# State-space recurrence: rows spread eight at a time from blocks laid out by GpSimd, squares and end scaling on ScalarE, inputs over three segments

## The reference, cut to what matters

```python
def step(h, inp):
    dA_t, dB_t, x_t, C_t, t = inp
    h = h * dA_t + dB_t * x_t[:, :, None]
    nrm = jnp.sqrt(jnp.sum(h * h, axis=(1, 2), keepdims=True))
    fac = jnp.minimum(20.0 / (nrm + 1e-08), 1.0)
    h = jnp.where(t % 10 == 0, h * fac, h)
    y = jnp.einsum('bdn,bn->bd', h, C_t) + D_param * x_t
    return (h, y)
```

## Time and profile before

| | |
|---|---|
| device time, 3 runs | 6174.59, 6184.56 (median), 6189.38 us |
| the profiled execution | 6185.92 us, of which the core's span is 6184.0 us |
| granted TensorE clock over the span | 0.867 of 2.4 GHz |
| PE, PEld, DVE, ACT, POOL busy in the span | 81%, 52%, 52%, 48%, 31% |
| the recurrence | 4094.8 to 4634.6 us after the span's start, about 540 us |
| first scan, last scan (53 in all) start | 4112.03, 4599.13 us |

### The profile page before, as it was taken

One profiled execution on the slowest core, in us unless ns is written; L12 is line 12 of the kernel. 1 busy time (PEld: TensorE's weight loads), 2 busy tenths in 40 slices (PEclk: granted clock), 3 DMA queues, 4 the chain that ended last, 5 costly groups with the idle time before them and its releaser, 6 DMA issues. The chain is left out here.

```text
span 6184.0 us, 108311 instructions
## 1 busy us (share of the span) xinstructions
PE 5032.6 (81%) x39346; PEld 3240.5 (52%) x39346; DVE 3189.3 (52%) x6332; ACT 2957.8 (48%) x8829; POOL 1901.8 (31%) x2082
## 2 busy tenths in 40 slices
PE   3998598978878878878788788778989944787888
PEld 2664255756636546546456456458886632223433
DVE  5551354556546446455356366358875544562433
ACT  2442244547647657556467477355534412352421
POOL 0230000347637457367277187001112300000000
PEclk6999799999989989899899799776669966895888
DMA  1000000001101111111111011000000000000000
GB/s 48 2 1 4 19 10 16 1 14 39 47 19 41 40 29 36 35 34 35 31 39 41 25 40 41 32 1 1 1 1 5 1 3 4 10 4 29 4 0 7
DMA packets 34520, 122.70 MB, mean 20 GB/s; under 512 B 8484, under 2 KB 9512, under 8 KB 32424
## 3 DMA queue, kind: packets, MB, share of 16 engines
q1 hardware_dynamic: 33960, 115.42, 6.9%
HBM read 36.43 MB, written 1.05 MB: 6 GB/s over the span
## 5 line engine op out<-in xcount | busy, mean ns | idle before, releaser
L640 POOL MEMSET norm_eps<- 128x1 f32 x16 | 1.6, 99 | 1905.7 <-POOLq L116 1847.2
L2087 POOL TENSOR_TENSOR local_rot<-local_raw,local_cos 128x512 f32<-128x512 f32 x384 | 488.1, 1271 | 303.5 <-DVE local_raw L2131 303.5
L2090 POOL TENSOR_TENSOR local_other<-local_raw,local_sin 128x256 f32<-128x256 f32 x768 | 557.6, 726 | 60.2
L2029 ACT ACTIVATE ps<-ps,local_negmax 128x96 f32<-128x96 f32 x1536 | 489.2, 322 | 37.2 <-DVE local_negmax L2110 36.9
L1952 PE MATMUL ps<-arena,local_xs 128*128 128x512 f32 x768 | 447.4, 667 | 71.8 <-ACT local_xs L2009 52.0
L2093 POOL TENSOR_TENSOR local_rot<-local_rot,local_other 128x512 f32<-128x512 f32 x384 | 487.4, 1269 | 30.1
L2024 ACT ACTIVATE local_squares<-ps 128x512 f32<-128x512 f32 x384 | 230.8, 601 | 508.2 <-PE ps L1952 507.8
L2117 DVE TENSOR_REDUCE local_norm<-local_squares 128x8 f32<-128x512 f32 x384 | 263.2, 685 | 282.4 <-ACT local_squares L2024 282.4
L1940 PE MATMUL ps<-local_K,local_Q 64*64 64x96 f32 x6144 | 337.0, 249 | 0.0
L2029 ACT ACTIVATION_READ_ACCUMULATOR ps<-ps,local_negmax 128x1 f32 x1536 | 331.0, 215 | 0.0
L2519 PE MATMUL ps<-ssm_BC,const 32*128 32x40 f32 (+1 forms) x3584 | 297.8, 373 | 26.4 <-PEq L116 22.0
(11 more groups left out here) (499 smaller groups left out, 11465.9 us busy)
## 6 DMA issues: line engine op xcount, KB each, us to landing
local_V_span<-local_V SPq DMA_DIRECT2D x96, 384.0 KB, 4.0
local_V_span<-local_V SPq DMA_DIRECT2D x96, 256.0 KB, 3.5
arena<-in_L1f_a SPq DMA_DIRECT2D x7, 2176.0 KB, 8.2
local_V_span<-local_V SPq DMA_DIRECT2D x72, 128.0 KB, 2.3
arena<-in_L3f SPq DMA_DIRECT2D x1, 3460.0 KB, 11.6
arena<-in_L1f_f SPq DMA_DIRECT2D x6, 537.5 KB, 4.0
arena<-in_L0f SPq DMA_DIRECT2D x1, 2824.5 KB, 9.8
arena<-in_L0x SPq DMA_DIRECT2D x1, 2049.5 KB, 9.0
```

The lines of the kernel that those rows point to most:

```text
L2029: nc.scalar.activation(scores, scores, ACT.Exp, bias=m.negmax[:, s % 2, u:u + 1], accum_out=m.total[:, s % 2, u:u + 1])\
L2087: link(nc.gpsimd.tensor_tensor(rot, raw, m.cos[:, t, a * DH:(a + 1) * DH].unsqueeze(1) .broadcast_to([P, 8, DH]), ALU.mult))
L2090: link(nc.gpsimd.tensor_tensor(other[:, :, lo:lo + HALF], raw[:, :, HALF - lo:DH - lo], m.sin[:, t, a * DH + lo:a * DH + lo + HALF].unsque ...
```

## The change

1. Spreading. GpSimd lays out, per chunk, four blocks of 8 rows x 40 tokens (`own`): block (kind, h) holds row n of `BC` in partition n of each sequence's 32 and zeros elsewhere (a product of `BC` with `own_row`, a tiled identity of 32; both operands broadcast). A use is then 2 matmuls of 32 x 128 by 320 columns, with ones as weights, in place of 16 of 40 columns.
2. The squares go from VectorE to ScalarE (L2588 after), and so does the scaling of the ends by `fac` (L2602 after: 4 instructions of 32 elements, one for each sequence). VectorE computes the product of ends and first decay before the factor is known (`pre`, L2699 after) and multiplies it with `fac` afterwards (L2720 after).
3. The B uses are spread in steps 0, 0, 1, 2 and their 16 takes stand in steps 1, 2, 3 as 4, 6, 6 (before: 8 in step 2, 8 in step 3). The C uses are spread in steps 2 and 3, three in 3; ScalarE copies one in step 3 and three in step 0 of the next chunk (before: all four in step 3).
4. The decays of a chunk are made in quarters (8 Tanh, Exp of 1280, two small ones), one in each step, the first of chunk k+2 in step 3 of chunk k. Before they stood in one piece at the start of a chunk.
5. In step 0 the second weighing product stands behind the reduction, and y of half 0 waits for it as before. In the other steps both stand ahead of it, as before. The second y input reads, and the `y_ready` waits of takes, follow half by half.

The diff, cut to its core:

```diff
+    sq, scratch, pre = buf("sq", [P, B, DN]), buf("scratch", [P, B, DN]), buf("pre", [P, B, DN])
...
-        return {1: [("B", k + 1, 0, 0), ("B", k + 1, 0, 1)], 2: [("B", k + 1, 1, 0), ("B", k + 1, 1, 1)],
-                3: [("C", k + 1, h, p) for h in range(2) for p in range(2)]}.get(i, [])
+        return [(kind, k + 1, h, p) for kind, h, p in
+                {0: [("B", 0, 0), ("B", 0, 1)], 1: [("B", 1, 0)], 2: [("B", 1, 1), ("C", 0, 0)],
+                 3: [("C", 0, 1), ("C", 1, 0), ("C", 1, 1)]}[i]]
...
+    TAKES = 0, 4, 6, 6
...
         def _(pe):
...
-                        for n in range(HALF):
-                            for b in range(2):
-                                part = slice(32 * (2 * p + b), 32 * (2 * p + b) + 32)
-                                row = 32 * (2 * p + b) + ROWS.index(kind) * SSM_N + HALF * h + n
-                                mm = nc.tensor.matmul(rows(use)[:, b, n, :],
-                                                      core.ident[part, row:row + 1].broadcast_to([32, P]),
-                                                      BC[part, cols], start=True, stop=True)
+                        pe.wait_ge(own_ready, 4 * (j + 1))
+                        for b in range(2):
+                            part = slice(32 * (2 * p + b), 32 * (2 * p + b) + 32)
+                            mm = nc.tensor.matmul(rows(use)[:, b, :, :], core.c("ones")[part, :],
+                                                  own(kind, h)[part, :, 0:length(j)], start=True, stop=True)
...
         def _(act):
             for k in CHUNKS_ALL:
+                for i in range(4):
+                    s = segment(k, i)
+                    if s is not None:
+                        act.wait_ge(scanned, s + 1)
+                        nc.scalar.activation(sq[:, :, :], ends(k, i), ACT.Square, scale=1.0 / LIMIT).then_inc(sq_ready, 1)
+                    for use in copying(k, i):
...
+                    early = QUARTER // 2 if i == 0 and k >= 0 else QUARTER
+                    for j, q in decays(k, i):
+                        rates_of(j, q, range(QUARTER * q, QUARTER * q + early))
+                    if s is not None:
+                        act.wait_ge(fac_ready, s + 1)
+                        for b in range(B):
+                            nc.scalar.mul(ends(k, i)[:, b, :], ends(k, i)[:, b, :], fac[:, b:b + 1]).then_inc(scaled, 1)
+                    for j, q in decays(k, i):
+                        rates_of(j, q, range(QUARTER * q + early, QUARTER * (q + 1)))
+                        decays_of(j, q)
...
         def _(pool):
...
+                        for g in range(4):
+                            mine = slice(HALF * g, HALF * (g + 1))
+                            nc.gpsimd.tensor_tensor(own(ROWS[g // 2], g % 2)[:, :, 0:length(j)],
+                                                    BC[:, cols].unsqueeze(1).broadcast_to([P, HALF, length(j)]),
+                                                    core.c("own_row")[:, mine].unsqueeze(2)
+                                                    .broadcast_to([P, HALF, length(j)]), ALU.mult).then_inc(own_ready, 1)
...
         def _(dve):
...
-                        link(nc.vector.tensor_tensor_scan(states(k, i), rates, states(k, i), 0.0, ALU.mult, ALU.add))
-                        nc.vector.scalar_tensor_tensor(out=sq[:, :, :], in0=ends(k, i), scalar=LIMIT ** -2,
-                                                       in1=ends(k, i), op0=ALU.mult, op1=ALU.mult).then_inc(sq_ready, 1)
...
+                        nc.vector.tensor_tensor_scan(states(k, i), rates, states(k, i), 0.0, ALU.mult, ALU.add)\
+                          .then_inc(scanned, 1)
+                    weigh(kk, ii, 0)
+                    if i > 0:
+                        weigh(kk, ii, 1)
...
+                            link(nc.vector.tensor_tensor(pre[:, :, :], first[:, nk % 2, ni, :, :], ends(k, i), ALU.mult))
...
+                    if i == 0:
+                        weigh(kk, ii, 1)
...
-                        last = nc.vector.tensor_tensor(ends(k, i), ends(k, i),
-                                                       fac[:, :].unsqueeze(2).broadcast_to([P, B, DN]), ALU.mult)
...
+                            link(nc.vector.tensor_tensor(scratch[:, :, :], pre[:, :, :], fac[:, :].unsqueeze(2)
+                                                         .broadcast_to([P, B, DN]), ALU.mult))
```

More of the change, by code:

```diff
@@ L2414, in state_recurrence @@
     u = buf("u", [P, 2, B, 2, SSM_CHUNK])
-    sq, scratch = buf("sq", [P, B, DN]), buf("scratch", [P, B, DN])
+    sq, scratch, pre = buf("sq", [P, B, DN]), buf("scratch", [P, B, DN]), buf("pre", [P, B, DN])
+    parts = [core.sums[:, 2:4, :].rearrange("p a b -> p (a b)")[:, g * HALF * SSM_CHUNK:(g + 1) * HALF * SSM_CHUNK]
+             for g in range(3)] + [buf("own", [P, HALF * SSM_CHUNK])[:, :]]
     half = buf("half", [P, B])
@@ L2525, in _ @@
         def _(act):
-            for k in CHUNKS_ALL:
[L2527 to L2543, removed]
-                    nc.scalar.copy(first[:, j % 2, 0:segs_of[j], :, :], starts).then_inc(first_ready, 1)
-                    act.wait_ge(first_ready, 2 * j + 1)
-                    nc.scalar.mul(starts, starts, 0.0).then_inc(first_ready, 1)
-                for use in spreading(k, 3):
-                    kind, j, h, p = use
-                    act.wait_ge(spread[kind], place(use) + 1)
-                    if j >= 2:
-                        act.wait_ge(weighed, 2 * segs_before[j - 1])
-                    nc.scalar.copy(C_rows[j % 2][:, 2 * p:2 * p + 2, HALF * h:HALF * (h + 1), 0:length(j)], rows(use))\
-                      .then_inc(copied, 1)
@@ new lines, in rates_of @@
+            def rates_of(j, q, ms):
+                if q == 0 and j >= 2 and 0 in ms:
+                    act.wait_ge(scanned, segs_before[j - 1])
+                cols = slice(SSM_CHUNK * j, SSM_CHUNK * j + length(j))
+                for m in ms:
+                    nc.scalar.activation(dA[j % 2][:, 0:segs_of[j], :, m, :].rearrange("p s b t -> p b s t"),
+                                         by_segment(dt[:, :, m // SSM_N, cols]), ACT.Tanh, scale=rate[:, m:m + 1])\
+                      .then_inc(tanh_ready, 1)
@@ new lines, in weigh, with take @@
+                dve.wait_ge(scaled, B * (s + 1))
+                part = H[:, k % 2, i, :, c * SSM_N:(c + 1) * SSM_N, :]
+                nc.vector.tensor_tensor(part, part, C_rows[k % 2][:, :, :, i * SEG:(i + 1) * SEG], ALU.mult)\
+                  .then_inc(weighed, 1)
+            def take(use, c, b):
+                kind, j, h, p = use
+                dve.wait_ge(spread["B"], place(use) + 1)
+                if h == 0 and p == 0:
+                    dve.wait_ge(u_ready, j + 1)
+                if h == 0 and j >= 2:
+                    dve.wait_ge(y_ready, 2 * (j - 2) + c + 1)
+                lo = c * SSM_N + HALF * h
+                nc.vector.tensor_tensor(H[:, j % 2, 0:segs_of[j], 2 * p + b, lo:lo + HALF, :]
+                                        .rearrange("p s n t -> p n s t"),
+                                        u[:, j % 2, 2 * p + b, c, 0:length(j)].unsqueeze(1)
+                                        .broadcast_to([P, HALF, length(j)]).rearrange("p n (s t) -> p n s t", t=SEG),
+                                        rows(use)[:, b, :, :].rearrange("p n (s t) -> p n s t", t=SEG),
+                                        ALU.mult).then_inc(taken, 1)
@@ L2621, in _ @@
                     s = segment(k, i)
+                    kk, ii = before(k, i)
                     if s is not None:
@@ L2643, in _ @@
                                                            op0=ALU.mult, op1=ALU.add).then_inc(y_read, 1)
-                    if s is not None:
-                        dve.wait_ge(norm_ready, s + 1)
-                        nc.vector.tensor_reduce(sums[:, :], NORM.rearrange("p (b n) -> p b n", b=B), AX_X, ALU.add)\
-                          .then_inc(norm_read, 1)
-                    taking(k, i)
+                    for use, c, b in taking_of(k, i):
+                        take(use, c, b)
                     if s is not None:
```

112 lines of the change are left out of this document (64 added, 48 removed).

## The result

The changed kernel takes 6134.35 us (median of 4 runs, 6131.06 to 6139.83) against 6186.64 before: 0.992 of it, 95% interval 0.9903 to 0.9937. The forecast was 6178, with a range from 6144 to 6206.

| us | before | after | difference | forecast |
|---|---|---|---|---|
| first L2398 after the stage's start to the first scan | 21.05 | 22.84 | +1.8 | +2.2 |
| chunk 0 | 36.17 | 36.23 | +0.1 | +2.5 |
| chunks 1 to 11, each | 37.90 | 34.28 | -3.62 (11 times: -39.8) | -0.66 |
| of it step 0 | 10.24 | 8.61 | -1.63 | +0.07 |
| step 1 | 7.74 | 8.37 | +0.63 | +1.6 |

The account below looks back on a forecast made before the run. It took VectorE to bound steps 1 to 3 and TensorE's queue step 0. First scan +2.2, chunk 0 +2.5, eleven chunks -7, chunk 12 -3, end -2.3: -7.6 on 6185.92 gives 6178 us, range 6144 to 6206.

Parts of the forecast that it names:

- Turn by turn: block 1 to 7.85, `scratch` 8.24, block 2 9.06, add 9.45, block 3 10.27.: Step 0 after the factor: GpSimd's blocks at 0.82 us alternate with VectorE's instructions; scan of step 1 at 10.3, was 10.23.
- Eight passes are 2.25.: Step 1, the two B uses behind y on TensorE: eight 320-column passes at 0.28 us each, done at 16.2.
- 7.25 us over 16 passes.: Trace row read as 0.45 us per 512-column pass, from which 0.28 us for a 320-column pass was taken.
- Block 4 takes its turn to 13.95, so the reduction is at 16.5.: Step 1: block 4 follows the scan ending at 13.1, B uses wait for it; step 1 costs 9.3 us, before 7.73.
- Steps 2 and 3: Each loses square, end scaling and two takes and gains `pre`; together 2.3 us less, 17.65 a chunk.
- ScalarE: Its scalings and decays end at 22.1, before the scan's end at 22.45, so it was costed at nothing.
- The edges: Outside chunks 1 to 11: first scan +2.2 us, chunk 0 +2.5, chunk 12 -3, the end -2.3.
- 1: Rival: the scan leaves the port free, so blocks 3 and 4 run beside it; -24 us, 6154; chance 0.20.
- 2: Rival: products aren't held at all; chunk near 34 us, 6140; chance 0.08.
- 3: Rival: a block costs 1.27 us, as GpSimd's 512-element product does; +22 us, 6200; chance 0.13.
- 4: Rival: TensorE stays at 1.2 GHz, its work broken by waits for blocks; +19 us, 6197; chance 0.17 together with 5.
- 5: Rival: ScalarE is late by 0.35 us in three steps a chunk; +13 us, 6191; chance 0.17 together with 4.

Follow-up runs that it names:

- e1: Changed kernel with the four block products left out from the third chunk on; chunk 34.01 us against 34.28, median 6136.27 us.
- e2: Changed kernel with each of the four block products made twice; chunk 38.52 us against 34.28, median 6192.56 us.
- e10: Changed kernel with its four block products a chunk, all spreads read from 128 partitions; chunk 35.75 us, median 6159.74 us.
- e8: e4 with every wide spread read from all 128 partitions in place of 32; chunk 32.84 us against 34.16, median 6115.59 us.
- e9: e4 with only the C uses read from 128 partitions, the B uses from 32; chunk 32.82 us, median 6123.05 us.
- e4: Changed kernel with one block product a chunk in place of four, the spread's weights picking the group of eight; chunk 34.16 us, median 6138.7 us.
- e6: Changed kernel without blocks, each use again 16 matmuls of 40 columns; chunk 39.22 us, median 6198.02 us.
- e11: e9 with the block and `u` made two chunks ahead, in step 2 behind the root; chunk 32.12 us, median 6111.72 us.

## Why the prediction was wrong, step by step

- **What bounds the kernel.** Right, and the stall of 1.82 us in step 0 went. That the next bound of step 1 is TensorE's queue was in the prediction too; it took it for longer than it is. In ten of the eleven chunks VectorE comes to the reduction of step 1 without idling; TensorE bounds it only once VectorE is faster (e1). Of the 3.0 us by which a chunk was forecast too long, 1.7 are in step 0, 0.9 in step 1 and 0.3 in steps 2 and 3.
- **Step 0 up to the factor.** Right within 0.1: reduction 4.17 (4.24 measured), second weighing product to 5.19 (5.26), root to 6.20 (6.14), `u` to 6.99 (6.92), factor to 7.03 (6.95).
- **"Turn by turn: block 1 to 7.85, `scratch` 8.24, block 2 9.06, add 9.45, block 3 10.27."** The first step that failed, by 1.7 us a chunk. The turns are there (the three waits in the chunk above, e2, e10), but a block and a product take about 0.73 together and not 0.82 + 0.39. My reading of it is that the duration shown for an instruction alone holds fixed parts beside its use of the port, and that these ran beside the other engine's turn: the factor, 0.16 alone, shows 0.78 beside `u` of 0.81, and `scratch`, issued 0.31 into a block, ends 0.87 behind the block's start. The earlier trace rows had this: 2.23 for a pair of 1.55 with a gate product between them (0.88 where it runs beside takes) is 0.68 more, not 0.88. That growth was measured; that fixed parts are its reason was not tested by itself.
- **"Eight passes are 2.25."** The second failed term: they take 0.82, 1.4 less. In the forecast's own sum this is worth 0.65, since VectorE's 15.85 then ends last and not 16.5. From 128 partitions eight take 2.31 (e8). From 32 those of different row groups run at the same time: one use, four passes in two row groups, takes 0.81, and two uses, eight passes in four row groups, take 0.82. By the Trainium skill, "TensorE: Matmul & The Clock Gate", Packing small matmuls, matmuls of 32 rows in different row groups run concurrently; the traces agree (0.82 against 2.31), and the prediction went halfway.
- **"7.25 us over 16 passes."** A misreading that did no harm. The row has 11 passes in 7.25 us, at a granted clock of 0.68; all 16 take 9.40. At 2.4 GHz four of them take 1.71, 0.43 each, so the 0.45 and the 0.28 for a pass from 128 rows came out right by luck.
- **"Block 4 takes its turn to 13.95, so the reduction is at 16.5."** The wait was right in kind: the block ends 0.5 behind the scan. But with the scan of step 1 at 8.61 it is done at 12.25. In the chunk shown y ends at 12.7, so TensorE does not wait. In chunks 1 to 3 y ends at 11.3 to 11.4 and TensorE waits for the block until 12.4, but the reduction stays at 14.0, since VectorE is not ready sooner. Take the cover away and the forecast step appears: 10.08 in e10, where 9.3 was said.
- **Steps 2 and 3.** -2.3 forecast, -2.62 measured; `scratch` with a broadcast factor takes 0.29, not 0.39, in each of the two steps. The last 0.1 stays open.
- **ScalarE.** "It fits by 0.35": it waits 0.46 for the scan in steps 2, 3 and 0; four scalings take 1.08. At the scan of step 1, which the forecast did not work out, it has nothing to spare: the decays end at 4329.70, the scan at 4329.65.
- **The edges.** The first scan and the end were right (+1.8 for +2.2, -2.2 for -2.3). Chunk 0, +0.1 for +2.5, failed mostly by the first term: from its first reduction to the next scan are 3.87 us and not 5.45. Chunk 12's -3.0 is as forecast by luck: step 0 gave 2.1 us where its terms, three short blocks among them, come to 1.1, steps 2 and 3 gave 1.4 where 2.3 was said.
- **Rivals.** 1 is refuted, since the scan is held 0.31 by the block under way when it is issued, and a block issued behind it ends 0.5 after it. 2 gave 6140 and "near 34" a chunk and so came near the result, for a wrong reason: products are held, but for less, and most of it lies in TensorE's shadow (e1). 3 is refuted: 0.72 a block. 4 had the clock at 0.50 in y, which is so, but y rises out of it as before; the clock was not a loss but an unused gain, 1.3 a chunk (e9). 5: the square of step 1 is late by 0.6 to 0.9 us wherever step 0 has no block or one and ScalarE's work is not evened (e1, e4, e6, e8, e9, e11), but it cost time only in e11.

Put the measured 34.3 in place of 37.25 in eleven chunks and +0.1 for chunk 0, and 6178 falls by 34.9 to 6143. The rest is the 9.7 outside the stage, which no term of the forecast had. The recurrence alone brings the time to the lower edge of the range (6144), and the rest below it.

## What to carry to other kernels

Where two engines take turns at a port, price a turn by the growth of the pair in the trace, not by adding the durations that both show alone. Work out every queue that meets at the next wait: a term on one of them is worth only what it is later than the other (1.46 us of waits were worth 0.27). And where TensorE works in short pieces, read the granted clock at the start of its next long piece: dearer passes ahead of it (2.31 for 0.82) made the whole faster.

## What the runs showed of the hardware that I had not expected

- Eight passes of 320 columns, 32 rows each, over four row groups: 0.82 us at 2.4 GHz; the same from 128 rows: 2.31.
- A product of GpSimd (0.72 to 0.82 us) delays VectorE's products and scans of two SBUF inputs by 0.3 to 0.5 us each, a `tensor_scalar` of 4 elements by 0.62, and takes with one input in PSUM by nothing. Broadcast operands or full ones make no difference (748 and 751 ns).
- With 12 spread passes of 128 rows in step 3 (5.2 us) TensorE begins y at 2.4 GHz, with the same passes of 32 rows (3.0 us) at 1.2: 4.61 against 7.3 us.
